# One core, LoRA layer and state-space convolution: where the fourth x sum is kept, and where filter and weight steps stand

## The reference, cut to what matters

```python
# layer 0: dense layer with a low-rank adapter chosen per sample (rank 16), residual
result = einsum('bsd,od->bso', x, base_weight) + base_bias      # 1024 x 1024
h = einsum('bsd,brd->bsr', x, lora_A_w[ids])
x = x + result + einsum('bsr,bor->bso', h, lora_B_w[ids])
# layer 1: per head a causal convolution of length 1024 with a filter K(h, l), residual
Ct = Cc * (exp(dtA) - 1) / A
K = 2 * real(einsum('hn,hnl->hl', Ct, exp(dtA * l)))            # 64 states per head
y = irfft(rfft(x, 2048) * rfft(K, 2048))[..., :1024] + x * D
x = x + y * (arange(1024) < length[b])
```

## Time and profile before

| | us |
|---|---|
| median of 3 runs (1111.36 to 1113.01) | 1111.9 |
| the profiled execution itself | 1110.41 |
| its span, first to last instruction | 1108.7 |
| TensorE busy, matmuls (97% of the span) | 1073.3 |
| TensorE not busy | 35.4 |
| VectorE busy (78%) | 864.9 |
| ScalarE busy (64%) | 714.8 |
| mean granted TensorE clock | 0.991 |

### The profile page before, as it was taken

How to read it: one execution, slowest core, us unless ns; L and a number is a source line. 1 busy time by engine, 2 the same in 40 slices (tenths; PEclk the granted TensorE clock), 3 DMA queues, 4 the chain that set the end, 5 groups by cost and what they waited for, 6 DMA issues and landing times.

```text
span 1108.7 us, 21535 instructions
## 1 busy us (share of the span) xinstructions
PE 1073.3 (97%) x8088; PEld 1038.4 (94%) x8088; DVE 864.9 (78%) x1279; ACT 714.8 (64%) x1260; POOL 27.5 (2%) x79
## 2 busy tenths in 40 slices
PE   9899999999989999899999799999999999999998
PEld 8799999999989999799999799999979999999997
DVE  6796887878778877778787788768568888888886
ACT  4664453673564854646745647556388888888885
POOL 0000000000000000000000000000000000000000
PEclk9899999999989999999999999999999999999999
DMA  7656778787768788687877687868699797889773
GB/s 244 247 182 241 216 244 270 248 263 225 262 187 287 225 266 264 178 274 240 287 221 263 176 287 247 265 232 265 257 284 357 276 349 280 337 285 349 283 275 133
DMA packets 162586, 284.62 MB, mean 257 GB/s; under 512 B 10739, under 2 KB 125620, under 8 KB 149044
## 3 DMA queue, kind: packets, MB, share of 16 engines
q1 hardware_dynamic: 162484, 283.26, 75.4%
HBM read 193.96 MB, written 89.26 MB: 255 GB/s over the span
## 4 chain that ended last, share of the span: by engine, by line
PE 73%; DVE 12%; DMA 6%; ACT 5%; SPq 2%; issue 2%; DVEq 0%; ACTq 0%
PE acc L1769 25%; PE acc L1929 24%; PE acc L1775 12%; PE acc L1697 4%; DMA x_scratch<-x_sb 4%; PE acc L1741 3%; PE acc L1964 3%; DVE x_lo L1073 2%; DMA u_raw<-x_scratch 1%; PE acc L1707 1%; SPq L447 1%; DVE t_lo L1073 1%; DVE b_st L1073 1%; ACT L848 1%; ACT L861 1%
## 5 line engine op out<-in xcount | busy, mean ns | idle before, releaser
L1073 DVE TENSOR_TENSOR t_lo<-t_raw,t_hi 128x1024 fp32r<-128x1024 f32 x63 | 77.1, 1224 | 102.5 <-ACT t_hi L690 101.8
L1929 PE MATMUL acc<-u_hi,f_hi 128*128 128x512 f32 (+1 forms) x320 | 129.0, 403 | 1.2 <-DVE u_lo L1073 1.2
L1769 PE MATMUL acc<-t_hi,w_pair 128*128 128x256 f32 x960 | 122.8, 280 | 4.4 <-ACT t_hi L690 4.1
L1769 PE MATMUL acc<-t_hi,v_lo 128*128 128x256 f32 x512 | 123.0, 279 | 0.0
L1769 PE MATMUL acc<-t_hi,v_hi 128*128 128x256 f32 x512 | 122.9, 279 | 0.0
L1769 PEld LDWEIGHTS acc<-t_hi,w_pair 128*128 128x128 f32 x960 | 116.9, 188 | 5.2 <-issue 5.2
L690 ACT ACTIVATE acc<-acc 128x512 f32<-128x512 f32 x93 | 53.2, 580 | 106.2 <-PE acc L1775 105.7
L1929 PE MATMUL acc<-u_lo,f_hi 128*128 128x512 f32 (+1 forms) x320 | 118.3, 370 | 0.0
L1929 PE MATMUL acc<-u_hi,f_lo 128*128 128x512 f32 (+1 forms) x320 | 118.2, 369 | 0.0
L1769 PE MATMUL acc<-x_hi,w_pair 128*128 128x256 f32 x720 | 97.2, 289 | 14.3 <-ACT acc L690 13.2
L1769 PEld LDWEIGHTS acc<-x_hi,w_pair 128*128 128x128 f32 x720 | 91.6, 196 | 15.6 <-ACT acc L690 13.8
(11 more groups left out here) (210 smaller groups left out, 2665.7 us busy)
## 6 DMA issues: line engine op xcount, KB each, us to landing
w_pair<-weight_scratch SPq DMA_DIRECT2D x71, 1024.0 KB, 6.0
x_scratch<-x_sb SPq DMA_DIRECT2D x32, 1024.0 KB, 6.1
out<-out_sb SPq DMA_DIRECT2D x63, 512.0 KB, 4.9
x_raw<-x_t SPq DMA_DIRECT2D x15, 2048.0 KB, 7.9
u_raw<-x_scratch SPq DMA_DIRECT2D x14, 2048.0 KB, 12.2
wq_raw<-state_scratch SPq DMA_DIRECT2D x16, 1024.0 KB, 7.6
a_raw<-lora_a SPq DMA_DIRECT2D x128, 64.0 KB, 1.9
b_raw<-lora_b SPq DMA_DIRECT2D x128, 64.0 KB, 2.1
```

The lines of the kernel that those rows point to most:

```text
L1073: return dve.tensor_tensor(dst, src, r32(hi), ALU.subtract)
L1769: pe.matmul(by_row(bank_part(bank, i)), w[:, k, i, :], hi[:, k, :, :], start=opens and i == 0 and k == 0 and s == 0, stop=False, skip_grou ...
L1929: mm = pe.matmul(bank, w, m, start=first and i == 0, stop=last and i == 2, skip_group_check=onto_closed)
```

## The change

Six things, in the words of the code: T4 = x21 - T2 in one operation, written for every group to `t4_raw`, a view of x_lo, whose quarter (0, 1) only `adapters_down` reads, and computed directly behind t2, in front of `split_t(T2)`; filter units at every place from group 2 on (one extra, in group 5), with the preparing steps one place earlier, and ScalarE's place 1 moved behind the split of the next x; in group 0 the odd weights' loads in front of the adapters' and their sums in front of `split_b`; in group 1 the x load in front of two weight stores, the even sums behind the split of x; at the seam u's first load earlier, `take_p5(0)` behind the first u splits, and ScalarE's order over heads 0 and 1 written out with state 1 earlier.

```diff
-    t4_at = work_at + 2 * V_BYTES
-    t4_first = place("t4_first", [P, HALF, heads, GH], F32, at=t4_at)
+    t4_raw = place("t4_raw", [P, NT, N], F32, at=x_lo_at)
...
     def t_source(g, n):
-        return t4_first[:, :, :, :] if g == 0 and n == "T4" else t_raw[:, :, :, LO_SLOT[n], :]
+        return block(t4_raw, 0, 1) if n == "T4" else t_raw[:, :, :, LO_SLOT[n], :]
...
-    UNIT_PLACES = [(2, PER_GROUP - 1)] + [(g, i) for g in range(3, LAST)
-                                          for i in range(PER_GROUP + (1 if g in (5, 8, 11) else 0))]
+    UNIT_PLACES = [(g, i) for g in range(2, LAST) for i in range(PER_GROUP + (1 if g == 5 else 0))]
@@ SyncE @@
             load_w(1)
+            load_v(v_raw[:, A11, :, :, :], 0, 0, ld_v11)
+            load_v(v_raw[:, A22, :, :, :], 1, 1, ld_v22)
+            load_v(a21_raw[:, :, :, :], 1, 0, ld_v21)
             sp.wait_ge(ld_ids, 16)
...
                 load_b(i, row)
-            load_v(v_raw[:, A11, :, :, :], 0, 0, ld_v11)
-            load_v(v_raw[:, A22, :, :, :], 1, 1, ld_v22)
-            load_v(a21_raw[:, :, :, :], 1, 0, ld_v21)
...
             load_blocks()
+            load_x(1)
+            store_x1(0, 0)
             store_plain(A11, 0)
             store_plain(A12, 1)
-            load_x(1)
-            store_x1(0, 0)
...
-                if g == 3:
-                    load_zb(0)
                 filter_stores(g, 0)
                 if g < LAST:
                     load_x(g + 1)
                 else:
                     store_unit(ALL_UNITS - 1)
+                    for par in range(2):
+                        sp.wait_ge(st_x1[par], 16 * g)
+                    sp.wait_ge(c_t["T4"], n_groups)
+                    load_u(0, LAST)
...
                 if g == 2:
                     store_exponents()
+                    load_zb(0)
@@ ScalarE @@
-                if g == 1 and place == 2:
+                if g == 1 and place == 1:
                     filter_pre()
...
             split_b(0)
+            split_v(A11)
             take_h(0)
             split_h(0)
-            split_v(A11)
...
-            split_even(S2)
             take_p5(1, 0)
...
                 seed_b(0, g)
+                if g == 1:
+                    split_even(S2)
                 split_t(g, "T2")
...
                     split_a(g + 1)
-                filter_step(g, 1)
                 seed_e(0, g)
                 seed_e(1, g)
                 split_t(g, "T4")
...
                     take_p5(0, g)
                     for t in range(HALF, NT):
                         split_x(g + 1, t)
+                    filter_step(g, 1)
                 else:
-                    take_p5(0, g)
                     split_filter(0)
                     split_u_early(0)
+                    take_p5(0, g)
                     split_filter(1)
...
+            take_state(0, 0)
+            split_filter(2)
+            take_state(0, 1)
+            split_states(0, 0, 2)
+            take_state(0, 2)
+            split_states(0, 2, 3)
+            take_state(1, 0)
+            split_u_early(2)
+            split_u_late(2)
+            residual_late(0)
+            residual_late(1)
+            take_state(1, 1)
@@ VectorE @@
+            def weight_sum_4():
                 dve.wait_ge(ld_v12, 16)
...
             def split_x(g, t):
+                if g > 0 and t == 0:
+                    dve.wait_ge(c_tlo["T4"], g)
...
             def t4(g):
-                t = t_source(g, "T4")
-                if g > 0:
-                    dve.wait_ge(m_p6[1], g + 1)
-                link(dve.tensor_tensor(t, x_block(1, 0), x_block(1, 1), ALU.subtract))
-                dve.tensor_tensor(t, t, t_source(g, "T1"), ALU.add).then_inc(c_t["T4"], 1)
+                dve.wait_ge(m_h, g + 1)
+                dve.wait_ge(c_t["T2"], g + 1)
+                dve.tensor_tensor(t_source(g, "T4"), x_block(1, 0), t_source(g, "T2"), ALU.subtract).then_inc(c_t["T4"], 1)
...
+                if g == 1 and place == 1:
+                    filter_exponents()
                 if g == 1 and place == 2:
-                    filter_exponents()
+                    filter_quotients()
+                    filter_ratio()
                 if g == 2 and place == 0:
-                    filter_quotients()
+                    dve.wait_ge(c_elo, len(EVEN_ORDER))
                     filter_weights()
...
             t2(0)
-            t3(0)
+            weight_sums()
             split_b(0)
             keep_own(0)
             split_h(0)
-            weight_sums()
+            split_v(A11)
+            weight_sum_4()
             split_v(A12)
             split_v(S2)
+            t3(0)
+            t4(0)
             split_t(0, "T2")
-            t4(0)
...
             split_v(A22)
-            even_sums()
             split_t(0, "T4")
             out_12(1, 0)
             for t in range(NT):
                 split_x(1, t)
+            even_sums()
             for g in range(1, n_groups):
                 t1(g)
                 out_22(1, g - 1)
                 t3(g)
                 t2(g)
+                t4(g)
...
                 if g == 1:
                     split_even(S1)
-                t4(g)
                 split_t(g, "T1")
```

More of the change, by code:

```diff
@@ L650, in _ @@
                 load_filters(0)
-                for par in range(2):
-                    sp.wait_ge(st_x1[par], 16 * g)
-                sp.wait_ge(c_t["T4"], n_groups)
-                load_u(0, LAST)
                 for p in range(2):
@@ L1029, in _ @@
                 split_u_late(h)
-            for h in range(heads):
+            take_state(0, 0)
[10 more added lines that the diff above has]
+            take_state(1, 1)
+            split_states(1, 0, 2)
+            split_u_early(3)
+            split_u_late(3)
+            take_state(1, 2)
+            split_states(1, 2, 3)
+            split_filter(3)
+            for r in range(2, 4):
+                residual_early(r)
+                residual_late(r)
+            for h in range(2, heads):
                 ahead = h + 2 < heads
-                if 0 < h < EARLY - 2:
+                if h < EARLY - 2:
                     split_u_early(h + 2)
                     split_u_late(h + 2)
-                elif ahead and h > 0:
+                elif ahead:
                     split_u(h + 2)
                 take_state(h, 0)
-                if h == 0:
-                    split_filter(2)
-                elif h == 1:
-                    for r in range(2, 4):
-                        residual_early(r)
-                        residual_late(r)
-                elif h < EARLY - 2:
+                if h < EARLY - 2:
                     residual_early(h + 2)
@@ L1050, in _ @@
                 split_states(h, 0, 2)
-                if h > 0 and ahead:
+                if ahead:
                     split_filter(h + 2)
@@ L1054, in _ @@
                 split_states(h, 2, 3)
-                if h == 0:
-                    split_u_early(2)
-                    split_u_late(2)
-                    residual_late(0)
-                    residual_late(1)
         @blk.vector
@@ L1117, in weight_sums @@
             def weight_sums():
-                a11, a12, a22 = (v_raw[:, j, :, :, :] for j in (A11, A12, A22))
-                a21 = a21_raw[:, :, :, :]
+                a11, a22, a21 = v_raw[:, A11, :, :, :], v_raw[:, A22, :, :, :], a21_raw[:, :, :, :]
                 corner_residual(A11, ld_v11, 1)
@@ L1125, in weight_sums @@
                 v_sum(S2, v_raw[:, S1, :, :, :], a11, ALU.subtract, 5)
-                split_v(A11)
+            def weight_sum_4():
                 dve.wait_ge(ld_v12, 16)
-                v_sum(S4, a12, v_raw[:, S2, :, :, :], ALU.subtract, 6)
+                v_sum(S4, v_raw[:, A12, :, :, :], v_raw[:, S2, :, :, :], ALU.subtract, 6)
             def split_v(j):
@@ L1330, in filter_quotients, with filter_ratio @@
                 link(dve.reciprocal(k["inv"], k["t1"]))
-            def filter_weights():
-                lo_half, hi_half = slice(0, n_state), slice(n_state, P)
+            def filter_ratio():
                 mul("t1", "ni", "aim")
@@ L1343, in filter_weights @@
                 mul("qi", "t1", "inv")
+            def filter_weights():
+                lo_half, hi_half = slice(0, n_state), slice(n_state, P)
                 mul("t1", "cre", "qr")
@@ L1465, in filter_step @@
             def filter_step(g, place):
+                if g == 1 and place == 1:
+                    filter_exponents()
                 if g == 1 and place == 2:
-                    filter_exponents()
+                    filter_quotients()
+                    filter_ratio()
                 if g == 2 and place == 0:
-                    filter_quotients()
-                if g == 2 and place == 1:
-                    keep_exponents()
+                    dve.wait_ge(c_elo, len(EVEN_ORDER))
                     filter_weights()
@@ L1474, in filter_step @@
                     make_diag()
```

(4 more changed lines are left out.)

1 line of the change is left out of this document (removed).

## The result

The changed kernel takes **1120.7 us** (median of 6 runs, 1119.23 to 1125.99), the kernel before 1111.5 beside it (6 runs, 1109.72 to 1113.01): a ratio of 1.0090, 95% interval 1.0068 to 1.0112. It is slower by about 9 us. The forecast was 1114.3 with a range of 1098 to 1123. The profiled execution took 1122.24 us with a span of 1120.5, 11.8 more than the span before. First lines of the page of the changed kernel: busy time by engine, and from the costliest groups TensorE's two that wait (busy, mean ns | idle before, by releaser).

The account below looks back on a forecast made before the run. TensorE was taken as the bound. Terms: -6.8 start, +1.5 group 1, -28.8 old stalls, +34.2 new wait, +0.5, -2.0 seam, +3.8 clock = +2.4; 1110.41 becomes 1112.8, plus 1.5 for the median: 1114.3 us, range 1098 to 1123.

Parts of the forecast that it names:

- the wait costs more: Rival: all stalls of kinds 0, 3, 4 drop the clock (+16), or out_12(1) is late (+3): 1118 to 1133, chance 0.12.
- kinds 0 and 3: Filter steps in VectorE's place 0: stalls of 3.1 (0; 4.5 in group 2) and 3.9 (3; 1.3 more in group 6).
- kind 4: VectorE filter step, e unit after e unit, in place 0 of groups 5, 8, 13: stalls of 2.3 us each.
- The new wait: VectorE, groups 2 to 14: t4 waits for m_h ahead of the T2 split, delaying end_11 and p3: 34.2 us of stalls.
- kind 1: Filter step finishing the factors, no ScalarE part, in place 0 of groups 4, 7, 12: stalls of 2.1 us each.
- kind 2: Filter step of 3.78 us on VectorE, in place 0 of groups 9 and 14: stalls of 0.2 us each.
- The 28.8 go in full: Groups 2 to 14: all 28.8 us lost in the kernel before vanish through the new placing of filter units and place 1.
- The rival in which the wait costs nothing: VectorE's chain has unseen slack, so the stalls and clock falls do not come: 1076 us, chance 0.08.
- Clock: TensorE: 1.5 falls to half clock after the stalls of groups 2 and 6, +3.8 us, between 0 and 20.
- The start: Group 0 to group 1: p1(0,1) at 59.3 instead of 66.11, so -6.8 us, between -4 and -7.7.
- Group 1 and group 15: Group 1: even sums before t1 delay p3, +1.5 us (0.5 to 3); group 15: later take_h costs 0.5.
- The seam: Before the second stage: earlier u load and ScalarE's state 1 cut TensorE's idle, -2.0 us (-2.5 to +1).

Follow-up runs that it names:

- experiment 11: Kernel of experiment 10 with t4 back in front of split_t(T2) and filter place 0 behind it, as in the changed kernel: 1122.8 us.
- experiment 2: Changed kernel with filter place 0 moved in front of t4 on VectorE, the wait kept: 1092.8 us, ratio 0.9833.
- experiment 8: Kernel of experiment 2 with the fourth filter unit moved from group 5 to group 14: 1097.9 us.
- experiment 9: Kernel of experiment 2 with group 2's filter_weights, make_diag and first unit in place 1, place 0 empty, an extra fourth unit in group 14: 1099.1 us.
- experiment 5: Changed kernel with unused matmuls filling TensorE's stalls before end_11 and p3 in groups 3, 6, 10 and 11: 1116.9 us.
- experiment 6: Kernel of experiment 2 with ScalarE's filter place 1 back in front of seed_e: 1092.8 us, ratio 0.9811.
- experiment 7: Kernel of experiment 2 with the filter units placed as in the kernel before, fourth units in groups 5, 8 and 11: 1100.7 us.
- experiment 10: Kernel of experiment 9 with the fourth units in groups 5 and 13 instead of 5 and 14: 1090.7 us.
- experiment 3: Kernel before with the T4 part alone: one operation into x_lo's quarter behind t2, waiting for m_h: 1126.2 us, ratio 1.0133.

## Why the prediction came out right, point by point

The sign and the mechanism were right: the wait holds VectorE's chain. One term was much too small, one cause was put down wrongly without harm to the sum, and two gains were smaller than forecast; the time came 6.4 us above the forecast, inside its range. It did not come in the 1111 to 1119 that the forecast itself was given, but in the 1118 to 1133 of the rival "the wait costs more", which had a chance of 0.12. Its condition was half met: the clock fell in all five groups of kinds 0 and 3 and in none of kind 4, so it cost 9.1 us more than forecast, not 16.

- **The new wait.** t4 at A+3.95 and `keep_own` at A+11.71 for kind 3 (forecast 11.70) are as worked out. The idle times by kind of place 0 were 3.5 for kind 3 (forecast 3.9), 2.8 for kind 0 (3.1), 1.9 for kind 1 (2.1), 1.8 for kind 4 (2.3) and none for kind 2, the same in the changed kernel and, in other groups without a fourth unit before them, in experiment 11. What groups 2 to 14 lose without the falls of the clock: 32.4 us (29.2 of it in idles over 0.3 us) against 34.2. Experiments 2 and 11 show the cause by one moved line. That VectorE keeps its order while an operation waits (the Trainium skill, "TensorE: Matmul & The Clock Gate", section "Architectural detail: the array is 16× 32×32, not 1× 128×128") the trace bears out: the T2 split, whose high part ScalarE had ready at 169.43, stood until 174.77 behind t4's 5.29 us of idle time.
- **The rest behind the wait** was put down wrongly: "The 28.8 go in full". The rival in which the wait costs nothing was given 1076, and without the wait the kernel takes 1093 to 1097. In groups 2 and 6 I charged 9.7 us to the wait; 13.5 are lost there with place 0 in front of it (experiment 2). Group 2's own place 0 and the fourth unit of group 5 do it (experiments 8 and 9). In the changed kernel wait and placing delay the same B split, so the losses overlap instead of adding up: group 2 loses 6.7 us with the wait and 5.7 without it, group 6 7.7 with and without. That the sum was spared is luck.
- **Clock: the mis-sized term.** Forecast 1.5 falls of 2.5 us, 3.8. Measured: five falls in groups 2, 3, 6, 10 and 11, 12.9 us above their idle times, 2.6 each; some of this is not the clock, since the groups without a fall take 0.2 to 0.7 us above their idle times too. The price was about right and the number wrong. I took it that idles of 2 us and less are harmless, and wrote that no idle between 1.20 and 4.08 us was seen, where before has two of 1.44 and 1.45 (groups 9 and 12, `end_11`), both at full clock; in groups 3, 10 and 11 two such idles (1.7 and 1.8, or 1.4 and 1.4) with 1.2 us busy between dropped the clock, and in experiment 5 a single one of 1.81 did. The bounds given for this term, 0 to 20, held it.
- **The start**: -4.9 at group 1 against -6.8. TensorE idled 2.11 us at 35.04 waiting for hl, which no row of before had shown it do, and ran at half clock from there: the next matmuls stand 0.21 us apart. p1 began at 36.79 instead of 35.0, and again at 61.23 instead of 59.3. Eight experiments (2 and 5 to 11) have the same start. In the seven where the clock did not fall there (idles of 1.2 to 2.0 us) `adapters_down` of group 1 begins at 65.0 to 66.0, in the eighth, with 2.39 us and a fall, at 67.15; so without the fall the start is worth 5.8 to 6.8, and most of what is missing is the clock's again.
- **Group 1 and group 15**: 1.2 against 1.5, and 0.1 against 0.5. In group 1 the size was near for another reason: the idle, 0.90 us, is at `end_11` for the B split, and p3, where I had put it for S4, did not wait.
- **The seam**: -1.0 against -2.0. The 1.20 us went, but at 831.58 TensorE waits 2.07 for ScalarE's state copy, as in every variant with this seam; before, there were two waits of 1.3 together.

Together, from the span of before: -4.9 + 1.2 + 16.4 + 0.1 - 1.0 = 11.8, where 16.4 is 32.4 + 12.9 - 28.9 in groups 2 to 14. The forecast's terms give 2.4; the 1.5 us it added for the median went the other way, the profiled execution being 1.6 above the median of after. The 9.4 between them are 9.1 of clock, 1.9 of the start and 1.0 of the seam, less 1.8 of stalls, 0.7 in groups 1 and 15, and 0.1 because 28.9 went instead of 28.8.

By measured kernels the parts are worth: the T4 part +16 alone (experiment 3), and +28 to +32 behind the new placing, where nothing else hides it; the new placing -6 to -8; the start -5 to -7 at group 1 with the earlier x load. Not settled is what decides whether an idle of 1.4 to 2.2 us drops the clock, and, within the spread of the runs, whether place 1's move is worth the 3 us that the rows show.

## What to carry to other kernels

Moving an operation that waits for another engine to the front of an in-order list costs what stands behind it, not what the operation takes: look for independent work of the idle's length to put in front of it, which here made 30 us of difference. When a stall is taken away, ask which other chain ends next at the same place, because two causes of one late operation do not add up, neither in the loss nor in the gain. Count short stalls as clock risks too: here two of 1.4 to 1.8 us in a row cost 1.6 to 1.8 times their length where the clock fell.

## What the runs showed of the hardware

- A TensorE idle of 1.81 us, with TensorE busy around it, was followed by the 1.2 GHz level in experiment 5 (16 products in 3.6 us) and not in the changed kernel (2.13 us), in the same place of the same group. In all thirteen traces each of TensorE's 25 idles of 2.4 us and more had the 1.2 GHz level in it or within 1.1 us of its end; of idles between 1.4 and 2.2 us some had and some had not, and the same idle of 2.07 us at the seam did in five of ten kernels. In the changed kernel a fall cost 1.8 to 3.1 us beyond the idle itself.
- The clock goes with the spread of one kernel's times: experiment 2 took 1088.8 us in a run with a mean clock of 0.997 and 1094.7 in one with 0.992. Experiment 10 had 0.997 or 0.998 in each run and a spread of 2.8 us. Experiment 7, with three idles of 4.5 us and half clock behind each, had 0.989 to 0.991 and the narrowest spread, 1.3 us.
